# Output projection of a state-space scan: one fp32 product becomes three products of split operands, and its weights are streamed

## The chip, the cores and the metric

One core of one Trainium2 chip runs the whole kernel. The metric is the device time in microseconds (us), measured over several executions; beside it stands one execution taken by the hardware profiler. The engines are named as in the profile: PE is TensorE (matmuls; PEld is its weight load), DVE is VectorE, ACT is ScalarE, POOL is GpSimd, SP is SyncE, which here only issues transfers (DMAs).

## What is computed

A decoder layer on 2048 tokens (8 sequences of 256) with 256 channels: a Mamba-2 mixer, cross attention, and a mixture of experts. The change touches the mixer alone. Cut to what matters:

```python
proj = hidden @ W_in.T                      # z, x, B, C, dt;  inner width 4096 (64 heads of 64)
xBC  = silu(causal_conv(xBC))               # 4 taps
y    = scan(x * dt, B, C, exp(cumsum(dt*A))) + D * x
g    = y * silu(z)                          # the gated product, [tokens, 4096]
gn   = g * rsqrt(mean(g*g) + eps) * norm_w  # norm_w: 4096 values
out  = gn @ W_out.T                         # the output projection, 4096 -> 256
```

The kernel multiplies norm_w into W_out, projects g without the norm, and scales the result by the rsqrt of each token at the end of a group of tokens.

## The kernel before

`mamba_prepare` normalises the input, computes dt and its cumulative sums, splits the input weights into two float32r parts (high and low: high is the rounded value, low the rest) and stores them in HBM. Its ScalarE also multiplies norm_w into the whole output weight, 32 pieces of 128x256 (`weigh_out`, L290), which then stays in SBUF as `won`.

`mamba_scan` works through 128 steps. A step n is one tile of 128 inner channels (c = n mod 32, two heads) for one group of 512 tokens (g = n div 32). Each engine has its order written out by hand; semaphores count what is done. In its step n an engine does the following, in this order.

- PE: `transposes(n)` (L892), `x_proj(n+2)` and `z_proj(n+1)` (L873, 12 float32r products of 512 columns), `out_proj(n-1)` (L917, 4 fp32 products of 256 columns, each issued as 2 instructions), `scan(n)` (L905, into `ps_y`).
- DVE: `gate(n-1)` (L817, y from PSUM, writes `gy`), `x_times_dt(n)` (L807), `conv_x(n+1)` (L776, three instructions), `matrices(n+1)` (L786 and L789: `mat` times `cbm`, both operands and the result in SBUF), `silu_x(n+1)` (L794), `silu_z(n+1)` (L801).
- ACT: `scale_x(n+1)` (L690), `gaps(n+2)` (L702 and L704, eight instructions), `tanh_x(n+1)` (L721), `square(n-1)` (L717), `tanh_z(n+1)` (L727), `decays(n+2)` (L711).
- POOL: waits for `matrices(n+1)`, then `last_matrix(n+1)` (L663), `product(n)` (L640, g = gy times zs, writes `gT`), `add_square(n-1)` (L651, sums g*g; for the first tile of a group it is a copy, L648).
- SP: loads of the split input weights (`w_split`, 512 KB) and of the decay rows (512 KB) three steps ahead.

All of POOL's operands lie in SBUF. Of DVE's instructions in a step, L786 and L789 alone read two operands from SBUF; the others read one of theirs from PSUM. At the turn of a group DVE and POOL also compute the rsqrt and add the 512 tokens' output to `xres` (L829). At the end of the last step DVE splits the query weights for the next phase (L855).

Of the kernel before, what the change touches and what calls it, by code (L numbers as in the profile page):

```python
# [5 lines left out]
F32 = mybir.dt.float32  # L6
# [56 lines left out]
def mamba_prepare(nc, xres, ident, raw, banks, scratch, kept, first, x, w_xz, w_bc, w_dt, conv_w, conv_b, dt_bias, a_log, d_param, norm_w, w_out):  # L63

    xT_hi, xT_lo, cbm, dt, cum, cw, cb, d_ch, won, neg_half, ones, a_dram, w_dram = kept
# [23 lines left out]
    with ExitStack() as ctx:  # L89
# [16 lines left out]
        nw = sb("nw", [P, NCT])  # L106
# [17 lines left out]
        def pb(name, banks=1):  # L124
# [7 lines left out]
        wdt_loaded, wbc_loaded, small_loaded, wo_loaded = (  # L132
            sem(n) for n in ("wdt_loaded", "wbc_loaded", "small_loaded", "wo_loaded"))
# [5 lines left out]
        small_hi, small_lo, won_done = sem("small_hi"), sem("small_lo"), sem("won_done")  # L139
# [34 lines left out]
        def _(sp):  # L174
            x_t = x.rearrange("b (n p) c -> p (b n) c", p=P)
            for g in range(NG):
# [6 lines left out]
                     (nw[:], norm_w)]  # L183
# [9 lines left out]
            sp.dma_start(won[:], w_out).then_inc(wo_loaded, 16)  # L193
# [60 lines left out]
        def _(act):  # L254
# [32 lines left out]
            def weigh_out(c):  # L287
                if c == 0:
                    act.wait_ge(wo_loaded, 16)
                act.activation(won[:, c, :], won[:, c, :], ACT.Copy, scale=nw[:, c:c + 1]).then_inc(won_done, 1)  # L290

# [27 lines left out]
            for j in range(5, 9):  # L319
                for c in range((j - 5) * 8, (j - 4) * 8):  # L320
                    weigh_out(c)
                w_high(j)
            tanh(0)
            w_high(9)
            for n in range(2):
                act.wait_ge(aT_ready, n + 1)
                act.activation(aT[:, n * TG:(n + 1) * TG], ps_dt[:, n * TG:(n + 1) * TG], ACT.Copy)\
                    .then_inc(aT_done, 1)
# [217 lines left out]
def mamba_scan(nc, xres, ident, banks, scratch, kept, first, retired, next_loads, keys, split):  # L546

    xT_hi, xT_lo, cbm, dt, cum, cw, cb, d_ch, won, neg_half, ones, a_dram, w_dram = kept
# [3 lines left out]
    NCT = won.shape[1]  # L552
# [9 lines left out]
    TRI = 3 * P  # L562

    with ExitStack() as ctx:
# [7 lines left out]
        a_all = [a_first] + [sb(f"a_all{u}", [P, HPT, TG])[:] for u in range(1, 3)]  # L572
        mat = sb("mat", [P, 3, HPT, BG * TRI])
# [11 lines left out]
        def pb(name, banks=1):  # L585
# [9 lines left out]
        (x_scaled, gap_done, exp_done, x_tanh, z_tanh, g_squared) = (  # L595
            sem(n) for n in ("x_scaled", "gap_done", "exp_done", "x_tanh", "z_tanh", "g_squared"))
        mat_last = sem("mat_last")
        (conv_step, x_silu, z_silu, xdt_done, mat_done, gy_done, g_done, sum_mean, x_added) = (
            sem(n) for n in ("conv_step", "x_silu", "z_silu", "xdt_done", "mat_done", "gy_done", "g_done",
                             "sum_mean", "x_added"))  # L600
        (g_summed, r_veps, r_done) = (sem(n) for n in ("g_summed", "r_veps", "r_done"))
# [5 lines left out]

        block = ctx.enter_context(nc.Block())

        @block.sync  # L610
        def _(sp):
            sp.sem_clear(retired)
            for n in range(N):
# [6 lines left out]
                if n >= 3:  # L620
                    sp.wait_ge(gap_done, HPT * (n - 2))
                if n >= 1:
                    row = a_dram[g, c * HPT:(c + 1) * HPT, :].rearrange("h t -> (h t)")
                    sp.dma_start(a_all[u].rearrange("p h t -> p (h t)"), row.partition_broadcast(P))\
                        .then_inc(a_loaded[u], 16)
                if n == 8:
                    sp.wait_ge(w_stored[2], 16 * (NCT // 8))
                    sp.wait_ge(w_stored[3], 16 * (NCT // 8))
                    for dst, src, loaded in next_loads:
                        sp.dma_start(dst, src).then_inc(loaded, 16)  # L630

# [1911 lines left out]
```

## Time and profile before

| | before |
|---|---|
| median of 3 runs | 1694.83 us (1694.37 to 1695.42) |
| the profiled execution's own time | 1693.64 us |
| its span | 1691.9 us |
| busy share PE, DVE, ACT, POOL | 95%, 74%, 72%, 43% |

The span is what the profiler saw between the first and the last instruction, so 1.7 us of the profiled execution lie around it. The page divides the span into stages with quite different limits: about 86 us of `mamba_prepare`, 870 us of `mamba_scan`, then attention and experts. The shares above are means over all of them, so the argument has to be made inside the scan, and there inside one step.

### The profile page before, as it was taken

The page shows a single profiled execution, that of the slowest core. Times are in us where ns is not written, and L with a number is a line of the kernel's source. Part 1 is how long each engine was busy: PE and PEld are TensorE (multiplying, and loading weights), DVE is VectorE, ACT ScalarE, POOL GpSimd, SP SyncE. Part 2 cuts the span into 40 slices and gives each one's busy share as a digit, 9 for nine tenths or more (in the row PEclk, how much of TensorE's full clock was granted, in tenths as well). Part 3 has the DMA queues.
Part 4 walks back from the last instruction along what each step waited for, and adds up shares of the span by engine and source line. Part 5 has one row for each costly group of instructions (what it writes and reads, how often), then busy time and mean ns, then how long its engine had stood idle before and what let it go on. Part 6 is the DMA issues. An engine that isn't in the chain of part 4 may idle for free. (4 is left out here: it accounts for less than half of the span.)

```text
span 1691.9 us, 29098 instructions
## 1 busy us (share of the span) xinstructions
PE 1603.2 (95%) x9864; PEld 1281.0 (76%) x9864; DVE 1254.0 (74%) x2044; ACT 1217.1 (72%) x2518; POOL 731.8 (43%) x601
## 2 busy tenths in 40 slices
PE   5479999999999999999999999999969999999999
PEld 3357777777777777777777677878757889999888
DVE  7969999999999999999999865567666533333355
ACT  4679999999999999999999576566624324444331
POOL 1425555555555555555555511311113653334460
PEclk9689999999999999999999999999989999999999
DMA  8966444444444444444444100000215323222231
GB/s 324 389 231 253 164 152 172 150 158 167 151 172 152 154 171 150 173 151 153 172 150 150 55 1 13 14 14 14 72 75 190 117 96 133 90 91 95 79 99 51
DMA packets 78078, 226.62 MB, mean 134 GB/s; under 512 B 9072, under 2 KB 32880, under 8 KB 76272
## 3 DMA queue, kind: packets, MB, share of 16 engines
q1 hardware_dynamic: 72272, 198.67, 32.9%
q0 software_dynamic: 5664, 26.09, 4.4%
q8 instruction: 85, 1.39, 0.3%
q14 instruction: 57, 0.47, 0.1%
HBM read 187.77 MB, written 36.96 MB: 133 GB/s over the span
## 5 line engine op out<-in xcount | busy, mean ns | idle before, releaser
L776 DVE SCALAR_TENSOR_TENSOR m_xc<-banks,k_cw,m_xc 128x510 f32<-128x510 f32 (+2 forms) x384 | 285.4, 743 | 16.6 <-ACT m_xc L690 7.2
L917 PE MATMUL m_ps_out<-k_won,m_gT 128*128 128x256 f32 x1024 | 242.3, 379 | 3.2 <-POOL m_gT L640 2.0
L873 PE MATMUL banks<-pair_hi,m_wxz 128*128 128x512 f32 x680 | 241.7, 406 | 2.5 <-DMA m_wxz<-w_split 2.5
L640 POOL TENSOR_TENSOR m_gT<-m_gy,m_zs 128x512 f32<-128x512 f32 x128 | 166.4, 1300 | 172.3 <-DVE m_gy L817 171.4
L663 POOL TENSOR_TENSOR m_mat<-m_mat,k_cbm 128x384 f32<-128x384 f32 x128 | 129.8, 1014 | 230.6 <-DVE m_mat L789 216.8
L917 PEld LDWEIGHTS m_ps_out<-k_won,m_gT 128*128 128x128 f32 x1024 | 193.6, 190 | 36.1 <-POOL m_gT L640 3.3
L905 PE MATMUL m_ps_y<-m_mat,m_xdt 128*64 128x256 f32 (+1 forms) x2048 | 194.7, 332 | 0.0
L711 ACT ACTIVATE m_mat<-m_mat 128x1536 f32<-128x1536 f32 x128 | 188.6, 1473 | 0.0
L905 PEld LDWEIGHTS m_ps_y<-m_mat,m_xdt 128*64 128x64 f32 x2048 | 126.8, 136 | 80.0 <-issue 42.3
L702 ACT ACTIVATE m_mat<-m_a_all,k_cum 128x256 f32<-128x256 f32 x340 | 170.6, 502 | 0.0
L651 POOL TENSOR_TENSOR m_g_sum<-m_g_sum,m_g_sq 128x512 f32<-128x512 f32 x124 | 162.4, 1310 | 5.3 <-ACT m_g_sq L717 5.1
L873 PEld LDWEIGHTS banks<-pair_hi,m_wxz 128*128 128x128 f32 x680 | 127.6, 188 | 31.3 <-DMA m_wxz<-w_split 3.5
L2384 PE MATMUL f_gu<-f_room,f_gT_hi 128*128 x468 | 141.3, 363 | 2.4 <-issue 2.4
L2243 DVE TENSOR_TENSOR f_h<-f_silu,f_gu 128x256 f32<-128x256 f32 (+1 forms) x117 | 44.0, 376 | 129.7 <-PE f_ps_hT L2394 107.4
L817 DVE SCALAR_TENSOR_TENSOR m_gy<-m_xs,logits,m_ps_y 128x512 f32<-128x512 f32 x128 | 95.6, 747 | 55.1 <-PE m_ps_y L905 54.7
L873 PE MATMUL banks<-pair_lo,m_wxz 128*128 128x512 f32 x340 | 134.4, 395 | 0.0
L704 ACT ACTIVATE m_mat<-m_a_all,k_cum 128x128 f32<-128x128 f32 x340 | 134.1, 394 | 0.0
L873 PE MATMUL banks<-pair_hi,k_w_first 128*128 128x512 f32 x344 | 127.3, 411 | 3.8 <-PEq L89 2.5
L786 DVE TENSOR_TENSOR m_mat<-m_mat,k_cbm 128x768 f32<-128x768 f32 x128 | 121.4, 949 | 2.8 <-ACT m_mat L711 2.8
L1175 POOL TENSOR_TENSOR a_q_r<-a_q_ve,a_neg_half 128x32 f32<-128x32 f32 x8 | 43.4, 5426 | 168.9 <-DVE a_q_ve L1368 168.9
L2309 PE MATMUL f_gu<-pair_hi,f_room 128*128 128x512 f32 x320 | 104.7, 404 | 6.5 <-DVE f_room L2064 6.3
L690 ACT ACTIVATE m_xc<-banks,logits,k_cw 128x512 f32<-128x512 f32 x128 | 98.3, 768 | 8.9 <-PE banks L873 8.9
(325 smaller groups left out, 3774.9 us busy)
## 6 DMA issues: line engine op xcount, KB each, us to landing
m_wxz<-w_split SPq DMA_DIRECT2D x85, 512.0 KB, 3.4
m_a_all<-a_by_head SPq DMA_DIRECT2D x85, 512.0 KB, 4.4
k_w_first<-w_split SPq DMA_DIRECT2D x43, 512.0 KB, 3.3
k_a_first<-a_by_head SPq DMA_DIRECT2D x43, 512.0 KB, 4.2
w_split<-p_w_hl SPq DMA_DIRECT2D x15, 1024.0 KB, 8.6
raw<-in_w_gate_up POOLq DMA_DIRECT2D x9, 1280.0 KB, 6.5
raw<-in_w_xz SPq DMA_DIRECT2D x16, 512.0 KB, 7.1
raw<-in_w_down POOLq DMA_DIRECT2D x9, 640.0 KB, 7.9
```

Source lines behind the costliest of these rows:

```text
L640: pool.tensor_tensor(gT[:, n % 2, :], gy[:, n % 2, :], zs[:, n % 2, :], ALU.mult).then_inc(g_done, 1)
L651: pool.tensor_tensor(g_sum[:, g % 2, :], g_sum[:, g % 2, :], g_sq[:, n % 2, :], ALU.add)\
L663: pool.tensor_tensor(mat[:, n % 3, 1, TRI:2 * TRI], mat[:, n % 3, 1, TRI:2 * TRI], cbm[:, n // NCT * BG + 1, :], ALU.mult).then_inc(mat_la ...
L702: act.activation(mat[:, u, h, b * TRI:b * TRI + SEQ], a_all[u][:, h, b * SEQ:(b + 1) * SEQ], ACT.Relu, bias=cum[:, t, head:head + 1], scal ...
L704: last = act.activation(mat[:, u, h, b * TRI + SEQ:(b + 1) * TRI], a_all[u][:, h, b * SEQ + P:(b + 1) * SEQ], ACT.Relu, bias=cum[:, t + 1, ...
L711: act.activation(mat[:, n % 3], mat[:, n % 3], ACT.Exp, scale=-1.0).then_inc(exp_done, 1)
L776: dve.scalar_tensor_tensor(out=out[:, :, k:], in0=ps[:, :, 0:SEQ - k], scalar=cw[:, c, TAPS - 1 - k:TAPS - k], in1=out[:, :, k:], op0=ALU. ...
L786: dve.tensor_tensor(mat[:, u, 0, :], mat[:, u, 0, :], cbm[:, g * BG:(g + 1) * BG, :].rearrange("p b t -> p (b t)"), ALU.mult)\
L873: last = pe.matmul(ps[:, :], w, a, start=m == 0, stop=m == len(terms) - 1)
L905: last = pe.matmul(ps_y[h * HD:(h + 1) * HD, b * SEQ + at:(b + 1) * SEQ], xdt[:, 2 * b + half, h * HD:(h + 1) * HD], mat[:, u, h, b * TRI ...
L917: last = pe.matmul(ps_out[:, q * HID:(q + 1) * HID], gT[:, n % 2, q * P:(q + 1) * P], won[:, c, :], start=c == 0 and q % 2 == 0, stop=c == ...
L2384: last = pe.matmul(ps_gu[m % 4][:, 0:2 * (i1 - i0)], a, w, start=q == 0, stop=q == len(terms) - 1)
```

## The change

The output projection gets two float32r parts of each operand: g is split into `gT_hi` and `gT_lo`, and the weighted output weight into `won[..., 0]` (high) and `won[..., 1]` (low); the three products hi*hi, hi*lo and lo*hi replace the fp32 one. POOL makes both parts of g. The output weight no longer stays in SBUF: a ring of 4 tiles (`WON`) is kept. In the first group (steps 1 to 32) the raw weight tile is loaded, ACT makes the high part and DVE the low one, and SP stores both parts in HBM; in groups 1 to 3 SP streams both parts back (256 KB a step). `out_proj` moves from step n+1 to step n+2. The 32 weightings and the 4 MB load leave `mamba_prepare`. Several semaphores are merged, and a sign moves from ACT's `scale=-1.0` into the stored rows, which changes no instruction's size.

```diff
 mamba_prepare:
-            sp.dma_start(won[:], w_out).then_inc(wo_loaded, 16)
-                for c in range((j - 5) * 8, (j - 4) * 8):
-                    weigh_out(c)
 mamba_scan, sync:
+            def move_won(n):
+                kept_c, c = n - WON - 2, n - WON
+                if n > WON:
+                    sp.wait_ge(won_moved, 16 * won_moves(n - 1))
+                if 0 <= kept_c < NCT:
+                    sp.wait_ge(won_lo_done, kept_c + 1)
+                    sp.dma_start(won_dram[kept_c], won[:, kept_c % WON]...)
+                if 0 <= c < NCT:
+                    if c >= WON:
+                        sp.wait_ge(won_lo_done, c - WON + 1)
+                    sp.dma_start(won_raw[:, c % WON], w_out[:, c, :]).then_inc(won_moved, 16)
+                elif c >= NCT:
+                    sp.wait_ge(out_ready, c - WON + 1)
+                    sp.dma_start(won[:, c % WON]..., won_dram[c % NCT])
...
-                    sp.wait_ge(gap_done, HPT * (n - 2))
+                    sp.wait_ge(exp_done, n - 2)
...
+                if n >= WON:
+                    move_won(n)
 mamba_scan, gpsimd:
+            def high_part(n):
+                pool.wait_ge(g_done, n + 1)
+                if n >= 2:
+                    pool.wait_ge(out_ready, n - 1)
+                pool.tensor_copy(gT_hi[:, n % 2, :], gT[:, n % 2, :]).then_inc(gT_hi_done, 1)
+
+            def low_part(n):
+                pool.wait_ge(gT_hi_done, n + 1)
+                pool.tensor_tensor(gT_lo[:, n % 2, :], gT[:, n % 2, :], gT_hi[:, n % 2, :].bitcast(F32),
+                                   ALU.subtract).then_inc(gT_lo_done, 1)
...
                     last_matrix(n + 1)
+                if n >= 1:
+                    high_part(n - 1)
+                    low_part(n - 1)
                 if n < N - 1:
                     product(n)
...
                 if n == N - 1:
                     product(n)
+                    high_part(n)
 mamba_scan, scalar:
+            def won_high(c):
+                act.wait_ge(won_moved, 16 * won_moves(c + WON))
+                if c >= WON:
+                    act.wait_ge(out_ready, c - WON + 1)
+                act.activation(won[:, c % WON, 0], won_raw[:, c % WON], ACT.Copy, scale=nw[:, c:c + 1])\
+                    .then_inc(won_hi_done, 1)
...
-                if n == N - 1:
-                    wq_high()
-                if n >= 1:
-                    square(n - 1)
+                square(n - 1)
                 if n + 1 < N:
                     tanh_z(n + 1)
                 if n + 2 < N:
                     decays(n + 2)
+                if n <= NCT:
+                    won_high(n - 1)
+                if n == N - 1:
+                    wq_high()
 mamba_scan, vector:
+            def won_low(c):
+                dve.wait_ge(won_hi_done, c + 1)
+                dve.scalar_tensor_tensor(out=won[:, c % WON, 1], in0=won_raw[:, c % WON], scalar=nw[:, c:c + 1],
+                                         in1=won[:, c % WON, 0].bitcast(F32), op0=ALU.mult, op1=ALU.subtract)\
+                    .then_inc(won_lo_done, 1)
...
                     silu_z(n + 1)
+                if 1 <= n <= NCT:
+                    won_low(n - 1)
...
             wq_low(1, 0)
+            last_low_part()
             wq_low(1, 1)
 mamba_scan, tensor:
             def out_proj(n):
                 g, c = n // NCT, n % NCT
-                pe.wait_ge(g_done, n + 1)
+                pe.wait_ge(gT_lo_done, n + 1)
+                if g == 0:
+                    pe.wait_ge(won_lo_done, c + 1)
+                else:
+                    pe.wait_ge(won_moved, 16 * won_moves(n + WON))
...
+                terms = [(gT_hi, 0), (gT_hi, 1), (gT_lo, 0)]
                 for q in range(TPG):
-                    last = pe.matmul(ps_out[:, q * HID:(q + 1) * HID], gT[:, n % 2, q * P:(q + 1) * P],
-                                     won[:, c, :], start=c == 0 and q % 2 == 0, stop=c == NCT - 1,
-                                     skip_group_check=True)
+                    for m, (a, part) in enumerate(terms):
+                        last = pe.matmul(ps_out[:, q * HID:(q + 1) * HID], a[:, n % 2, q * P:(q + 1) * P],
+                                         won[:, n % WON, part], start=c == 0 and q % 2 == 0 and m == 0,
+                                         stop=c == NCT - 1 and m == len(terms) - 1, skip_group_check=True)
...
-                if n >= 1 and not turned:
-                    out_proj(n - 1)
+                if n >= 2 and not turned:
+                    out_proj(n - 2)
```

The order on POOL, in one step of the scan (the difference, the step before with - and the changed step with +; the waits stand in brackets):

```order
-L663 TENSOR_TENSOR m_mat<-m_mat,k_cbm 128x384 [waits m_exp_done,m_mat_done]
-L640 TENSOR_TENSOR m_gT<-m_gy,m_zs 128x512 [waits m_out_ready,m_g_squared,m_z_silu,m_gy_done]
-L651 TENSOR_TENSOR m_g_sum<-m_g_sum,m_g_sq 128x512 [waits m_g_summed,m_g_squared]
...
+L694 TENSOR_TENSOR m_mat<-m_mat,k_cbm 128x384 [waits m_exp_done,m_mat_done]
+L684 CAST k_gT_hi<-m_gT 128x512 [waits m_out_ready,m_g_done]
+L688 TENSOR_TENSOR k_gT_lo<-m_gT,k_gT_hi 128x512 [waits m_gT_hi_done]
+L660 TENSOR_TENSOR m_gT<-m_gy,m_zs 128x512 [waits m_gT_lo_done,m_g_squared,m_silu_done,m_gy_done]
+L671 TENSOR_TENSOR m_g_sum<-m_g_sum,m_g_sq 128x512 [waits m_g_summed,m_g_squared]
```

Two instructions, the cast and the subtraction, stand between `last_matrix` and `product` in every step.

The order on ACT in a step of the first group, from the last of the `gaps` on, in the changed kernel:

```order
L739 ACTIVATE m_mat<-m_a_all,k_cum 128x128
L763 ACTIVATE banks<-m_xc 128x512 [waits m_conv_step]
L759 ACTIVATE m_g_sq<-m_gT 128x512 [waits m_g_summed,m_g_done]
L769 ACTIVATE xn_ffn<-banks 128x512 [waits m_silu_done,m_z_ready]
L746 ACTIVATE m_mat<-m_mat 128x1536 [waits m_gap_done]
L752 ACTIVATE k_won<-k_won_raw,logits 128x256 [waits m_won_moved]
L725 ACTIVATE m_xc<-banks,logits,k_cw 128x512 [waits m_silu_done,m_x_ready]
```

The high part of the weight (L752) is the last thing of the step, behind `decays` (L746); before, `decays` was followed by the next step's `scale_x`.

The order on DVE at the same place, from the last instruction of the convolution to the first of the next one, in the changed kernel:

```order
L819 SCALAR_TENSOR_TENSOR m_xc<-banks,k_cw,m_xc 128x2x253 [waits m_conv_step]
L829 TENSOR_TENSOR m_mat<-m_mat,k_cbm 128x768 [waits m_exp_done]
L832 TENSOR_TENSOR m_mat<-m_mat,k_cbm 128x384
L837 SCALAR_TENSOR_TENSOR m_xs<-banks,m_xc 128x512 [waits m_tanh_done]
L844 SCALAR_TENSOR_TENSOR m_zs<-xn_ffn,banks 128x512 [waits m_g_done,m_tanh_done]
L865 SCALAR_TENSOR_TENSOR k_won<-k_won_raw,logits,k_won 128x256 [waits m_won_hi_done]
L860 SCALAR_TENSOR_TENSOR m_gy<-m_xs,logits,m_ps_y 128x512 [waits m_g_done,m_y_ready]
L850 TENSOR_TENSOR m_xdt<-banks,k_dt 128x512 [waits m_t_ready]
L819 SCALAR_TENSOR_TENSOR m_xc<-banks,k_cw,m_xc 128x2x255 [waits m_x_scaled]
```

The low part (L865) has come in between `silu_z` and `gate`, with a wait for ACT's L752; `gate`, `x_times_dt` and the next convolution are queued behind it. After step 32 the rows L752 and L865 are absent and the rest is as before.

## Rows read from the trace of the kernel before

**Rows 1.** The page's first lines: span, busy time and share of each engine.

```profile
span 1691.9 us, 29098 instructions
PE 1603.2 (95%) x9864; PEld 1281.0 (76%) x9864; DVE 1254.0 (74%) x2044; ACT 1217.1 (72%) x2518; POOL 731.8 (43%) x601
```

**Rows 2.** Busy time by stretch: prepare (two stretches), steady scan; count of instructions in brackets.

```profile
core 0: us, PE busy (x) PEld busy (x) DVE busy (x) ACT busy (x) POOL busy (x), PEclk, DMA share, GB/s
36.00:55.00 19.00, 2.06 (x9) 1.32 (x7) 18.62 (x17) 19.00 (x41) 0.00 (x0) 0.64 0.93 341
55.00:85.00 30.00, 19.67 (x62) 13.46 (x63) 26.33 (x40) 16.73 (x23) 19.88 (x9) 0.73 1.02 394
...
500.00:941.00 441.00, 439.97 (x2678) 339.08 (x2676) 404.99 (x610) 426.21 (x861) 238.03 (x204) 1.00 0.44 154
```

**Rows 3.** Timeline of PE in a steady step: start, duration, what.

```profile
603.36 1.89 PE L917 MATMUL m_ps_out<-k_won,m_gT 128*128 128x256 f32 x8
605.18 1.52 PE L905 MATMUL m_ps_y<-m_mat,m_xdt 128*64 128x256 f32 x16
```

**Rows 4.** Timeline of DVE in the same step; idle time and releaser in square brackets.

```profile
600.17 0.75 DVE L817 SCALAR_TENSOR_TENSOR m_gy<-m_xs,logits,m_ps_y 128x512 f32<-128x512 f32 x1 [0.48 <-PE m_ps_y L905]
...
601.44 2.30 DVE L776 SCALAR_TENSOR_TENSOR m_xc<-banks,k_cw,m_xc 128x510 f32<-128x510 f32 x3
603.65 0.95 DVE L786 TENSOR_TENSOR m_mat<-m_mat,k_cbm 128x768 f32<-128x768 f32 x1
604.52 0.55 DVE L789 TENSOR_TENSOR m_mat<-m_mat,k_cbm 128x384 f32<-128x384 f32 x1
...
606.75 0.75 DVE L817 SCALAR_TENSOR_TENSOR m_gy<-m_xs,logits,m_ps_y 128x512 f32<-128x512 f32 x1 [0.48 <-PE m_ps_y L905]
```

**Rows 5.** Timeline of ACT in the same step.

```profile
603.77 0.60 ACT L721 ACTIVATE banks<-m_xc 128x512 f32<-128x512 f32 x1
...
605.30 1.47 ACT L711 ACTIVATE m_mat<-m_mat 128x1536 f32<-128x1536 f32 x1
606.68 0.77 ACT L690 ACTIVATE m_xc<-banks,logits,k_cw 128x512 f32<-128x512 f32 x1
```

**Rows 6.** Timeline of ACT: `scale_x` of tiles 2, 3 and 32.

```profile
110.56 0.76 ACT L690 ACTIVATE m_xc<-banks,logits,k_cw 128x512 f32<-128x512 f32 x1
116.88 0.77 ACT L690 ACTIVATE m_xc<-banks,logits,k_cw 128x512 f32<-128x512 f32 x1
...
307.94 0.77 ACT L690 ACTIVATE m_xc<-banks,logits,k_cw 128x512 f32<-128x512 f32 x1
```

**Rows 7.** Timeline of POOL in the steady step.

```profile
601.00 1.29 POOL L640 TENSOR_TENSOR m_gT<-m_gy,m_zs 128x512 f32<-128x512 f32 x1 [1.41 <-DVE m_gy L817]
602.25 1.29 POOL L651 TENSOR_TENSOR m_g_sum<-m_g_sum,m_g_sq 128x512 f32<-128x512 f32 x1
605.15 1.01 POOL L663 TENSOR_TENSOR m_mat<-m_mat,k_cbm 128x384 f32<-128x384 f32 x1 [1.61 <-DVE m_mat L789]
```

**Rows 8.** Timeline of DVE, then POOL, at the scan's start and end.

```profile
98.20 0.96 DVE L786 TENSOR_TENSOR m_mat<-m_mat,k_cbm 128x768 f32<-128x768 f32 x1 [0.72 <-ACT m_mat L711]
99.08 1.35 DVE L789 TENSOR_TENSOR m_mat<-m_mat,k_cbm 128x384 f32<-128x384 f32 x1
...
98.32 1.70 POOL L663 TENSOR_TENSOR m_mat<-m_mat,k_cbm 128x384 f32<-128x384 f32 x1 [12.05 <-ACT m_mat L711]
...
944.95 4.46 POOL L651 TENSOR_TENSOR m_g_sum<-m_g_sum,m_g_sq 128x512 f32<-128x512 f32 x2
```

**Rows 9.** Groups of POOL by line and shape: busy us, mean ns of one, idle before.

```profile
L1894 POOL CAST f_room<-raw 128x1280 fp32r<-128x1280 f32 x8 | 10.1, 1258 | 0.0
...
L648 POOL COPY m_g_sum<-m_g_sq 128x512 f32<-128x512 f32 x4 | 2.5, 618 | 0.0
```

**Rows 10.** Groups by line (ACT in prepare, DVE at turns); last row: timeline of PE.

```profile
L290 ACT ACTIVATE k_won<-k_won,p_nw 128x256 f32<-128x256 f32 x32 | 13.2, 508 | 0.0
...
L829 DVE SCALAR_TENSOR_TENSOR xres<-m_ps_out,m_r_out,xres 128x256 f32<-128x256 f32 x12 | 4.9, 474 | 0.0
...
1397.43 1.86 PEld L2404 LDWEIGHTS f_ps_y<-f_room 128*128 128x128 f32 x15
```

More of the change, by code:

```diff
@@ L131, in mamba_prepare @@
         x_loaded = [sem(f"x_loaded{g}") for g in range(NG)]
[L132 to L133 removed]
+        wdt_loaded, wbc_loaded, small_loaded = (
+            sem(n) for n in ("wdt_loaded", "wbc_loaded", "small_loaded"))
         w_loaded = [sem(f"w_loaded{u}") for u in range(RING)]
@@ L326, in _ @@
                 act.wait_ge(aT_ready, n + 1)
-                act.activation(aT[:, n * TG:(n + 1) * TG], ps_dt[:, n * TG:(n + 1) * TG], ACT.Copy)\
+                act.activation(aT[:, n * TG:(n + 1) * TG], ps_dt[:, n * TG:(n + 1) * TG], ACT.Copy, scale=-1.0)\
                     .then_inc(aT_done, 1)
@@ L630, in _ @@
                         sp.dma_start(dst, src).then_inc(loaded, 16)
+            for n in range(N, N + WON):
+                move_won(n)
         @block.gpsimd
@@ L720, in tanh_x @@
                 act.wait_ge(conv_step, (n + 1) * CONV)
-                act.activation(ps_x[n % 2][:, :], xc[:, n % 2, :], ACT.Tanh).then_inc(x_tanh, 1)
+                act.activation(ps_x[n % 2][:, :], xc[:, n % 2, :], ACT.Tanh).then_inc(tanh_done, 1)
             def tanh_z(n):
@@ L725, in tanh_z @@
                 if n >= 1:
-                    act.wait_ge(z_silu, n)
-                act.activation(thz, ps_z[:, :], ACT.Tanh, scale=0.5).then_inc(z_tanh, 1)
+                    act.wait_ge(silu_done, 2 * n)
+                act.activation(thz, ps_z[:, :], ACT.Tanh, scale=0.5).then_inc(tanh_done, 1)
             def wq_high():
@@ L837, in _ @@
             for n in range(N):
-                turned = n % NCT == 1 and n > 1
                 if n >= 1:
                     gate(n - 1)
-                if turned:
+                if n % NCT == 1 and n > NCT:
                     mean_out(n // NCT - 1)
@@ L845, in _ @@
                     conv_x(n + 1)
-                if turned:
+                if n % NCT == 2 and n > NCT:
                     add_out(n // NCT - 1)
@@ L953, in _ @@
                     context_keys(0)
-                turned = n % NCT == 1 and n > 1 or n == N - 1
-                if n >= 1 and not turned:
-                    out_proj(n - 1)
+                turned = n % NCT == 2 and n > NCT
+                if n >= 2 and not turned:
+                    out_proj(n - 2)
                 scan(n)
                 if turned:
-                    out_proj(n - 1)
+                    out_proj(n - 2)
                 if n % NCT == 0 and n > 0:
                     sums(n // NCT - 1)
+            out_proj(N - 2)
             context_keys(1)
+            context_keys(2)
             out_proj(N - 1)
             sums(NG - 1)
-            context_keys(2)
             context_keys(3)
@@ L973, in mamba_phase @@
     NH = 2 * NCT
+    WON = 4
     with ExitStack() as ctx:
```

121 lines of the change are left out of this document (67 added, 54 removed).

## Prediction, made before the changed kernel ran

> **What bounds the kernel now.** I began with the page's first lines [rows 1]. PE is busy 95% of the span, which suggests that cheaper products help; but the mean runs over stages with different limits, so I took busy time by stretch next. In the steady scan (the last of [rows 2]) PE is busy 439.97 of 441.00 us, ACT 426.21, DVE 404.99 and POOL 238.03. PE comes first, but ACT is 3% behind, and that is the room that a faster PE has.
>
> The timeline of one step says the same in detail. From gate to gate [rows 4] a step is 606.75 - 600.17 = 6.58 us. DVE's one idle time is 0.48 us, waiting for PE's scan. ACT's own length shows where nothing holds it up: at the scan's start `scale_x` follows `scale_x` after 116.88 - 110.56 = 6.32 us [rows 6]. So PE sets 6.57, ACT would set 6.32, and DVE without its wait 6.58 - 0.48 = 6.10. POOL has three instructions in a step and waits 1.41 and 1.61 us before two of them [rows 7]; what the reader is to see there is where the idle time lies. POOL ends `add_square` at 603.54, DVE runs its two `matrices` instructions from 603.65 to 605.07 [rows 4], POOL begins `last_matrix` at 605.15. POOL rests exactly while DVE multiplies two operands out of SBUF.
>
> That matters because the two engines do not run such work side by side. In the first step they met [rows 8]: L786 ran from 98.20 to 99.16, POOL's L663 was issued at 98.32 and took 1.70 instead of 1.01, ending 0.86 after L786; then L789, issued at 99.08, took 1.35 instead of 0.55 and ended 0.41 after L663 did. At the end of the scan, beside DVE's L855 (also two SBUF operands), two `add_square` took 4.46 us instead of 2.58. The blocked one starts when the other ends, and merely 0.14 or 0.15 us of its fixed time is hidden. Instructions of DVE with one operand in PSUM do not do this: L776 lies under POOL's L640 and L651 [rows 4, 7] at its usual 2.30 for three.
>
> The Trainium skill, page "SBUF — State Buffer", section "Who interferes with whom", has this as an exclusive lock on a shared pair of ports, taken by a DVE instruction with two SBUF inputs against a GpSimd instruction that reads SBUF. By that rule the new POOL work of this change isn't free however idle POOL looks; the rows above agree.
>
> **The change part by part.**
>
> *PE.* Removed: 8 instructions from 603.36 to 605.18, 1.82 us [rows 3]. Added: 12 float32r products of 256 columns. The same form runs in the experts' stage, 15 weight loads in 1.86 us, 0.12 each [rows 10], so 12 take about 1.45. PE gains 0.37 a step, down to 6.2. Since ACT needs 6.32, no more than 0.25 of it could ever show.
>
> *POOL, groups 1 to 3.* Added in every step: the cast and the subtraction. The cast of 512 columns isn't in the trace; the nearest rows are the copy of 512 (0.618) and the cast of 1280 (1.258) [rows 9], so 0.49 (in proportion) to 0.62; I take 0.62, the row of its own width. The subtraction is a product's form, 1.29. Now POOL's chain after `matrices` is longer than DVE's way to the next `matrices`. From the end of L789: `last_matrix` begins 0.08 later [rows 7, 4] and takes 1.01; the cast 0.62; the subtraction waits for the cast, which I put at the same 0.08, and takes 1.29; `product` and `add_square` 1.29 each. Instructions that follow without a wait start 0.04 before the end of the one ahead (602.25 against 602.29 [rows 7]), three times here. Sum 0.08 + 1.01 + 0.62 + 0.08 + 3 x 1.29 - 3 x 0.04 = 5.54. DVE's way from the end of L789 to its next L786 is 6.10 less the 1.42 of the pair (603.65 to 605.07), 4.68. So L786 is issued 0.9 us before POOL is done, under `add_square`, which began at 4.29, before it, and is blocked. L786 ends 0.95 - 0.14 = 0.81 after `add_square`, L789 0.47 later (605.07 - 604.60), and `last_matrix` waits for both. That closes a loop: 5.54 + 0.81 + 0.47 = 6.82 us, longer than PE's 6.57 now. Lost: 0.25 a step in 95 steps, 24 us. Both ends: nothing blocked gives 6.32, a gain of 0.25; a cast as slow as a two-operand instruction (1.29) gives 7.49, a loss of 0.92.
>
> By the Trainium skill's rule just named (the loser blocks for the whole of the other's instruction, nothing hidden) the loop would be 6.96, and 13 us more would be lost; rows 8 show the 0.14 hidden, so I leave it out.
>
> *The first group.* Here ACT makes the high part of the weight as the last thing of a step, DVE waits for it with the low part, and `gate`, `x_times_dt` and the next convolution are queued behind that wait. That is a loop through ACT and DVE. From the convolution's end (603.74 [rows 4]) to `tanh_x` 0.03, from there to the end of `decays`' slot 606.68 - 603.77 = 2.91 [rows 5], then the high part, 0.51 (L290 is the same work [rows 10]), and 0.05 to be seen: DVE can issue the low part at 3.50. It has two SBUF operands, 256 columns; nearest row L829, 0.47 [rows 10]. POOL's subtraction lies there: L789 ends 1.33 after the convolution, and by the sum above the subtraction ends 0.08 + 1.01 + 0.62 + 0.08 + 1.29 - 0.04 = 3.04 later, at 4.37, and began at 3.08, ahead of the low part. So this ends at 4.37 + 0.47 - 0.14 = 4.70; `gate` starts 0.08 earlier, the convolution 1.27 after `gate` (601.44 - 600.17), and takes 2.30: 8.19 us a step. Before, the same steps took (307.94 - 110.56) / 30 = 6.58 [rows 6]. Lost: 1.61 in 31 steps (the first one hides it behind ACT's prologue), 50 us. Without the block the low part ends at 3.97 and a step takes 7.46, still 0.88 more: 27 us. ACT's added 0.4 alone would give 6.72.
>
> *Prepare.* ACT loses 32 instructions, 13.2 us [rows 10], and the DMAs 4.2 MB. I cost this at nothing: in 36 to 55 us, where they ran, DVE is busy 18.62 of 19 us [rows 2] with the chain that ends this stage, and they lay beside it; in 55 to 85 it is busy 26.33 of 30. The DMA share is 1.02 there, so if transfers set the end, up to 4 us (DVE's idle time) could come back.
>
> *Streaming.* 256 KB a step more beside 1 MB, at a DMA share of 0.44 [rows 2]; SP issues up to two more transfers a step. Each has two steps to land. Nothing; if it were late, PE would wait in `out_proj`, with `scan` and then DVE's `gate` behind it.
>
> *Turns and tail.* At a turn DVE adds output, as before. After the last step the cast and subtraction of tile 126, the cast of 127 and a subtraction on DVE stand on the way to the last sum: 0.62 + 1.29 + 0.62 + about 0.7 = 3 us.
>
> Sum: 24 + 50 + 3 = 77 us on the profiled execution's 1693.64, 1771. The median of the runs is 1.2 higher: 1772.
>
> **The rivals.**
>
> *The low part isn't blocked in the first group* (POOL's subtraction comes after it): 7.46 a step, 1772 - 23 = 1749. For it: 0.4 us decide the order. Against it: POOL's chain starts at the same L789 and has fixed lengths.
>
> *No block at all in the steady steps* (it was seen in the first and the last steps alone, since POOL rested in the rest): 6.32 a step from 33 on, 24 us gained, 27 lost in the first group, 3 in the tail: 1701. Against it, rows 8.
>
> *Faster.* PE's gain shows and the first group costs nothing. The mechanism would be that DVE's wait for ACT's high part is covered: the low part needs to be ready when `silu_z` ends (2.5 after the convolution) and comes at 3.50, so 1.0 us would have to go. It decides when that gap and the block both fall away: 0.25 in 126 steps, 1695 - 31 = 1664.
>
> *POOL is slower still*: a cast at two-operand price, or blocks that also catch DVE between L786 and L789. From half of that, 0.3 a step, to all of it, 0.67, in 126 steps: 1810 to 1856.
>
> **How the numbers follow.** Forecast (both loops) 0.63, its own range 1755 to 1790; first group unblocked 0.13; no block 0.09; faster 0.05; slower still 0.10. Leaving out the last three would leave 0.24 outside, so the range takes in the lower part of the slower case and all of the second: 1743 to 1800. Times within 0.2% (3.4 us) can't be told from no change here. Of the 0.09 I give 0.03 to within and 0.05 to slower, 0.01 to faster. Slower 0.91, same 0.03, faster 0.06.
>
> **What would show it.** In the changed profile L829 (was L786) should take about 1.7 to 1.8 instead of 0.95, ending some 0.81 after POOL's L671; gate to gate 6.8 in the later groups, PE and ACT both with idle time, POOL busy some 85%. In the first group gate to gate 8.2, L865 taking about 1.2 with an idle time before it that ACT's L752 ends. PE's L980 should take 1.4 to 1.5 in all. Prepare should end within 4 us of where it did. I am wrong if L829 stays at 0.95 beside a busy POOL, if L865 is issued before POOL's L688, or if PE waits in `out_proj` for a transfer.

## The result, and the profile after

| | before | after |
|---|---|---|
| median (4 runs each) | 1694.6 us (1693.2 to 1695.4) | 1768.8 us (1768.1 to 1771.3) |
| profiled execution, its span | 1693.64, 1691.9 | 1771.26, 1769.5 |

The changed kernel is slower: ratio 1.0445, 95% interval 1.0432 to 1.0458. The page's first lines, to be held against [rows 1]:

```profile
span 1769.5 us, 30975 instructions
PE 1580.4 (89%) x10376; PEld 1293.7 (73%) x10376; DVE 1352.4 (76%) x2077; ACT 1219.8 (69%) x2518; POOL 964.8 (55%) x856
```

PE lost 23 us of busy time and POOL gained 233. DVE gained 98 us with only 33 more instructions. Of these, the 32 low parts of the weight are busy 36.3 us in all, about 1.15 us each. The largest share lies in an old instruction that takes longer: L829 is busy 191.8 us where L786, the same work, was busy 121.4. Busy time by stretch, as in [rows 2]:

```profile
core 0: us, PE busy (x) PEld busy (x) DVE busy (x) ACT busy (x) POOL busy (x), PEclk, DMA share, GB/s
36.00:55.00 19.00, 2.83 (x13) 1.94 (x11) 18.62 (x17) 7.86 (x9) 0.00 (x0) 0.71 0.88 315
...
500.00:941.00 441.00, 410.55 (x2855) 331.35 (x2852) 436.46 (x592) 415.38 (x838) 347.09 (x327) 1.00 0.56 194
```

In the steady scan DVE alone is busy nearly all the time (436.46 of 441 us, 99%). Its timeline shows why (compare [rows 4]):

```profile
680.02 0.73 DVE L860 SCALAR_TENSOR_TENSOR m_gy<-m_xs,logits,m_ps_y 128x512 f32<-128x512 f32 x1
...
683.48 1.75 DVE L829 TENSOR_TENSOR m_mat<-m_mat,k_cbm 128x768 f32<-128x768 f32 x1
685.16 0.54 DVE L832 TENSOR_TENSOR m_mat<-m_mat,k_cbm 128x384 f32<-128x384 f32 x1
...
686.82 0.73 DVE L860 SCALAR_TENSOR_TENSOR m_gy<-m_xs,logits,m_ps_y 128x512 f32<-128x512 f32 x1
```

POOL's timeline in the same step (compare [rows 7]):

```profile
679.92 0.62 POOL L684 CAST k_gT_hi<-m_gT 128x512 fp32r<-128x512 f32 x1
680.62 1.29 POOL L688 TENSOR_TENSOR k_gT_lo<-m_gT,k_gT_hi 128x512 fp32r<-128x512 f32 x1
681.87 1.30 POOL L660 TENSOR_TENSOR m_gT<-m_gy,m_zs 128x512 f32<-128x512 f32 x1
683.12 1.30 POOL L671 TENSOR_TENSOR m_g_sum<-m_g_sum,m_g_sq 128x512 f32<-128x512 f32 x1
685.78 1.00 POOL L694 TENSOR_TENSOR m_mat<-m_mat,k_cbm 128x384 f32<-128x384 f32 x1 [1.36 <-DVE m_mat L832]
```

L829 is issued at 683.48, while POOL's L671 runs until 684.42. It shows 1.75 us where the same instruction took 0.95 before, and ends at 685.23, 0.81 after L671. Gate to gate is 6.80 us. PE now waits 0.47 us for the transposes' operand, and its output projection runs from 682.86 to 684.37, where `scan` begins, 1.51 us:

```profile
679.55 0.66 PE L949 MATMUL banks<-ident,m_xs 128*128 128x128 f32 x4 [0.47 <-DVE m_xs L837]
...
682.86 0.39 PE L980 MATMUL m_ps_out<-k_won,k_gT_hi 128*128 128x256 f32 x2
...
684.37 1.52 PE L962 MATMUL m_ps_y<-m_mat,m_xdt 128*64 128x256 f32 x16
```

The first group is another loop. DVE's timeline there, from the last of a convolution to the next L829:

```profile
202.84 0.74 DVE L819 SCALAR_TENSOR_TENSOR m_xc<-banks,k_cw,m_xc 128x506 f32<-128x506 f32 x1
203.50 0.95 DVE L829 TENSOR_TENSOR m_mat<-m_mat,k_cbm 128x768 f32<-128x768 f32 x1
...
207.06 1.15 DVE L865 SCALAR_TENSOR_TENSOR k_won<-k_won_raw,logits,k_won 128x256 fp32r<-128x256 f32 x1 [0.95 <-ACT k_won L752]
208.13 0.74 DVE L860 SCALAR_TENSOR_TENSOR m_gy<-m_xs,logits,m_ps_y 128x512 f32<-128x512 f32 x1
208.78 0.68 DVE L850 TENSOR_TENSOR m_xdt<-banks,k_dt 128x512 f32<-128x512 f32 x1
209.38 2.30 DVE L819 SCALAR_TENSOR_TENSOR m_xc<-banks,k_cw,m_xc 128x510 f32<-128x510 f32 x3
211.60 0.95 DVE L829 TENSOR_TENSOR m_mat<-m_mat,k_cbm 128x768 f32<-128x768 f32 x1
```

POOL there:

```profile
206.63 1.29 POOL L688 TENSOR_TENSOR k_gT_lo<-m_gT,k_gT_hi 128x512 fp32r<-128x512 f32 x1
208.94 1.30 POOL L660 TENSOR_TENSOR m_gT<-m_gy,m_zs 128x512 f32<-128x512 f32 x1 [1.02 <-DVE m_gy L860]
```

DVE waits 0.95 us for ACT's high part, then the low part (L865) is issued 0.86 us before POOL's subtraction ends (207.92), takes 1.15 us and ends 0.29 after it. L829 is unblocked here, 0.95, since the delayed DVE gives POOL time to finish. A step is 8.10 us.

ACT's timeline, `scale_x` of tiles 2 and 32, says how much each part of the scan lost (compare [rows 6]):

```profile
111.34 0.76 ACT L725 ACTIVATE m_xc<-banks,logits,k_cw 128x512 f32<-128x512 f32 x1
...
352.76 0.77 ACT L725 ACTIVATE m_xc<-banks,logits,k_cw 128x512 f32<-128x512 f32 x1
```

Tile 2 comes 0.8 us later than before; from tile 2 to tile 32 it is 241.4 instead of 197.4 us, 44.0 more; from tile 32 to tile 127 654.8 instead of 628.9, 26.0 more (worked out from the starts of that instruction for the two tiles in each trace); and from there to the first instruction of the next phase on DVE 5.3 more. Together 76 of the 77.6 us by which the profiled executions differ; that of the changed kernel was the slowest of its four, and the medians differ by 74.2 us.

### The profile page after: what moved, and what is told of

Its sections match the earlier page's. It is cut to its first block and busy times, and to the rows that moved or that the text cites. A ratio compares the mean times of both kernels' runs of the same rounds, so it can differ in the third digit from the quotient of the medians.

```text
span 1769.5 us, 30975 instructions
## 1 busy us (share of the span) xinstructions
PE 1580.4 (89%) x10376; PEld 1293.7 (73%) x10376; DVE 1352.4 (76%) x2077; ACT 1219.8 (69%) x2518; POOL 964.8 (55%) x856
## 5 line engine op out<-in xcount | busy, mean ns | idle before, releaser
L980 PE MATMUL m_ps_out<-k_won,k_gT_hi 128*128 128x256 f32 x1024 | 188.8, 282 | 5.8 <-DVE k_gT_lo L872 2.6
L829 DVE TENSOR_TENSOR m_mat<-m_mat,k_cbm 128x768 f32<-128x768 f32 x128 | 191.8, 1498 | 2.8 <-ACT m_mat L746 2.8
L746 ACT ACTIVATE m_mat<-m_mat 128x1536 f32<-128x1536 f32 x128 | 188.6, 1474 | 0.0
L980 PEld LDWEIGHTS m_ps_out<-k_won,k_gT_hi 128*128 128x128 f32 x1024 | 166.4, 190 | 20.0 <-DVE k_gT_lo L872 3.5
L949 PE MATMUL banks<-ident,m_xs 128*128 128x128 f32 x512 | 85.2, 290 | 98.4 <-DVE m_xs L837 98.4
L688 POOL TENSOR_TENSOR k_gT_lo<-m_gT,k_gT_hi 128x512 fp32r<-128x512 f32 x127 | 164.6, 1296 | 10.2
L671 POOL TENSOR_TENSOR m_g_sum<-m_g_sum,m_g_sq 128x512 f32<-128x512 f32 x124 | 161.8, 1305 | 2.3 <-ACT m_g_sq L759 2.3
L949 PEld LDWEIGHTS banks<-ident,m_xs 128*128 128x128 f32 x512 | 54.8, 142 | 128.3 <-DVE m_xs L837 127.4
L980 PE MATMUL m_ps_out<-k_won,k_gT_lo 128*128 128x256 f32 x512 | 144.2, 282 | 0.0
```

What stands on the lines that cost most here:

```text
L671: pool.tensor_tensor(g_sum[:, g % 2, :], g_sum[:, g % 2, :], g_sq[:, n % 2, :], ALU.add)\
L688: pool.tensor_tensor(gT_lo[:, n % 2, :], gT[:, n % 2, :], gT_hi[:, n % 2, :].bitcast(F32), ALU.subtract).then_inc(gT_lo_done, 1)
L746: act.activation(mat[:, n % 3], mat[:, n % 3], ACT.Exp, scale=-1.0).then_inc(exp_done, 1)
L829: dve.tensor_tensor(mat[:, u, 0, :], mat[:, u, 0, :], cbm[:, g * BG:(g + 1) * BG, :].rearrange("p b t -> p (b t)"), ALU.mult)\
L949: last = pe.transpose(ps_t[:, q * P:(q + 1) * P], xs[:, n % 2, q * P:(q + 1) * P], ident)
L980: last = pe.matmul(ps_out[:, q * HID:(q + 1) * HID], a[:, n % 2, q * P:(q + 1) * P], won[:, n % WON, part], start=c == 0 and q % 2 == 0 an ...
```

## Experiments

All kernels start from the changed one unless the text says otherwise. The medians beside them are of 4 to 11 runs, against the kernel before on the same chip (1692.8 to 1694.9). Not all experiments ran on one chip, so a difference between two of them is good to about 1 us; the ratios leave the chip out.

**1. An operand from PSUM.** The kernel leaves out the multiplication by `cbm` from tile 34 on: DVE multiplies `mat` by what lies in a PSUM bank instead. Only the place of one operand is meant to change.

```diff
+                if n > NCT + 1:
+                    t_part = ps_t[:, 0:TRI]
+                    dve.tensor_tensor(batches(mat[:, u, 0, :]), batches(mat[:, u, 0, :]),
+                                      t_part.unsqueeze(1).broadcast_to([P, BG, TRI]), ALU.mult).then_inc(mat_done, 1)
+                    dve.tensor_tensor(mat[:, u, 1, 0:TRI], mat[:, u, 1, 0:TRI], t_part, ALU.mult)...
```

> From tile 34 on DVE's two matrices instructions read a PSUM bank in place of cbm (the result is wrong from there on), so they have one operand in SBUF; everything else, POOL's new work included, is as in the changed kernel. Theory (DVE's instruction with two SBUF operands and POOL's instructions exclude each other): the first of them takes 0.95 to 1.0 us again instead of 1.75 beside a POOL that is as busy as before, gate to gate falls from 6.81 to the lengths of PE and ACT, 6.32 to 6.40, in 94 steps: 1768.8 - 42 = 1727 (1722 to 1732). Rival (POOL's load slows DVE whatever its operands, or POOL's own chain of 5.5 us with its waits sets the step): the instruction stays at 1.7 or the step stays at 6.8, 1765 to 1770.

Measured 1729.6 us, ratio 1.0199 (1.0182 to 1.0216). DVE, then POOL, in its steady step:

```profile
682.67 0.94 DVE L831 TENSOR_TENSOR m_mat<-m_mat,banks 128x768 f32<-128x768 f32 x1
...
689.00 0.95 DVE L831 TENSOR_TENSOR m_mat<-m_mat,banks 128x768 f32<-128x768 f32 x1
```

```profile
681.98 1.30 POOL L671 TENSOR_TENSOR m_g_sum<-m_g_sum,m_g_sq 128x512 f32<-128x512 f32 x1
...
688.31 1.30 POOL L671 TENSOR_TENSOR m_g_sum<-m_g_sum,m_g_sq 128x512 f32<-128x512 f32 x1
```

The multiplication is again issued under POOL's L671 (682.67, while that runs until 683.28) and takes 0.94. The step is 6.33. POOL does the same work as in the changed kernel, 5.3 us a step in both. So it is not POOL's load as such nor the length of its chain that costs 0.47 us a step, but that DVE's instruction takes both operands from SBUF beside it.

**2. PE's part undone.** In groups 1 to 3 one fp32 product of the two high parts takes the place of the three; the products with the low parts are left out.

```diff
+                if g > 0:
+                    for q in range(TPG):
+                        last = pe.matmul(ps_out[:, q * HID:(q + 1) * HID], gT_hi[...].bitcast(F32),
+                                         won[:, n % WON, 0].bitcast(F32), ...)
```

> In groups 1 to 3 PE makes one fp32 product of the two high parts again instead of three (the low parts are still made, streamed and waited for, but not used, so precision is lost). That undoes PE's share of the change alone. Theory (POOL and DVE set 6.81): PE goes back to 6.57 of its own, its wait for the transposes' operand shrinks from 0.47 to 0.23, the step stays at 6.81 and the time at 1769 (1766 to 1772). Rival (PE's gain of 0.24 shows in the step and the new loop costs more than I think): 95 x 0.24 = 23 us slower, 1792.

Measured 1772.1 us (1767.7 to 1773.0), ratio 1.0446 (1.0429 to 1.0464), that of the changed kernel and at the upper end of the expected range. PE's output projection takes 1.82 us again and the step stays, at 6.79:

```profile
681.72 1.89 PE L980 MATMUL m_ps_out<-k_won,k_gT_hi 128*128 128x256 f32 x8
683.54 1.52 PE L962 MATMUL m_ps_y<-m_mat,m_xdt 128*64 128x256 f32 x16
```

The cheaper products were worth nothing in the kernel as changed.

**3. The whole of `mat` on DVE.** One instruction of 1536 columns replaces DVE's two and POOL's `last_matrix`. POOL begins its cast when it is over.

```diff
-                dve.tensor_tensor(mat[:, u, 0, :], ...)
-                dve.tensor_tensor(mat[:, u, 1, 0:TRI], ...)
+                cb_all = cbm[:, g * BG:(g + 1) * BG, :].rearrange("p b t -> p (b t)")
+                dve.tensor_tensor(mat[:, u], mat[:, u],
+                                  cb_all.unsqueeze(1).broadcast_to([P, HPT, BG * TRI]), ALU.mult)...
-                    pool.wait_ge(mat_done, HPT * (n + 2))
-                    last_matrix(n + 1)
+                        pool.wait_ge(mat_done, n + 2)
```

> DVE multiplies the whole of mat (128x1536) in one instruction and POOL's last_matrix is gone; POOL begins the cast when DVE's instruction is over. Theory (the sum of the work that excludes each other sets the step): POOL's chain falls from 5.54 to 4.53, the multiplication is issued 4.7 after the last one ended, so nothing blocks; it takes about 1.75, DVE alone is 6.10 + 0.33 = 6.43, and this is the step in groups 1 to 3, 6.4 to 6.5: 33 to 39 us back; in the first group 7.6 to 7.8 instead of 8.1, 10 to 15 us back. 1768.8 - 47 = 1722 (1714 to 1732). Rival (DVE has no idle time in the changed steady step, so DVE is the bound and takes on more work): 6.81 + 0.33 = 7.14, 1769 + 31 = 1800.

Measured 1713.1 us, ratio 1.0108 (1.0091 to 1.0125): DVE took on more work, and the kernel became 56 us faster. DVE and POOL in the steady step:

```profile
683.13 1.75 DVE L822 TENSOR_TENSOR m_mat<-m_mat,k_cbm 128x1536 f32<-128x1536 f32 x1
...
689.47 1.75 DVE L822 TENSOR_TENSOR m_mat<-m_mat,k_cbm 128x1536 f32<-128x1536 f32 x1
```

```profile
681.79 1.31 POOL L670 TENSOR_TENSOR m_g_sum<-m_g_sum,m_g_sq 128x512 f32<-128x512 f32 x1
684.94 0.61 POOL L683 CAST k_gT_hi<-m_gT 128x512 fp32r<-128x512 f32 x1 [1.84 <-DVE m_mat L822]
```

POOL has ended at 683.10, 0.03 before DVE begins: nothing blocks. The step is 6.34, below my 6.43; the DVE work of a step without any wait is a little shorter than the 6.10 that I had taken (without a wait an instruction's row begins 0.08 before the end of the one ahead). The time is 9 us better than expected and just below the range of 1714 to 1732: in the traces 41.7 us came back in groups 1 to 3 (33 to 39 expected) and 16.6 in the first group (10 to 15 expected). The rival, by which a DVE without idle time can't take on work, is out. A blocked instruction counts as busy: 0.8 us of DVE's busy time in each steady step of the changed kernel was waiting.

In the first group the step is 7.47. DVE, then POOL:

```profile
208.67 0.52 DVE L856 SCALAR_TENSOR_TENSOR k_won<-k_won_raw,logits,k_won 128x256 fp32r<-128x256 f32 x1 [0.61 <-ACT k_won L744]
```

```profile
207.62 1.29 POOL L687 TENSOR_TENSOR k_gT_lo<-m_gT,k_gT_hi 128x512 fp32r<-128x512 f32 x1
```

The low part is issued late in the subtraction, 0.24 before it ends, and takes 0.52 us, where it takes 0.48 by itself (experiment 8). So the block costs it 0.04 us at most, and the loop through ACT sets this step.

**4. The high part early.** ACT makes it right after `scale_x`.

```diff
                     scale_x(n + 1)
+                if n <= NCT:
+                    won_high(n - 1)
...
-                if n <= NCT:
-                    won_high(n - 1)
```

> ACT makes the high part of the weight right after scale_x instead of at the end of its step; all else as in the changed kernel. Theory (DVE's wait for ACT's last instruction closes the loop of the first group): the wait before L865 is gone, only its own 0.3 to 0.5 us stays in the loop of POOL and DVE, 6.81 + 0.35 = 7.15 (7.0 to 7.3) instead of 8.10 in some 29 steps: 28 us back, 1741 (1736 to 1746). Rival (the exclusion with POOL's subtraction costs the first group most of its time, wherever the high part is made): at best 0.3 of the 1.5 us comes back, 7.8, 1760. Groups 1 to 3 stay at 6.81 by both.

Measured 1759.1 us, ratio 1.0372 (1.0355 to 1.039): 10 us instead of 28. ACT's timeline shows a new wait:

```profile
208.34 0.51 ACT L752 ACTIVATE k_won<-k_won_raw,logits 128x256 fp32r<-128x256 f32 x1 [0.66 <-DMA k_won_raw<-in_w_out]
```

The load of a raw tile is the last that SP issues in a step, and at the start of ACT's next one it hasn't landed. The steps vary between 6.7 and 9.7 us, and one takes 13.7. The exchange of one wait for another decides nothing; hence the next experiment.

**5. The high part in the middle** of ACT's step, between `gaps` and `tanh_x`.

```diff
                     gaps(n + 2, 1)
+                if n <= NCT:
+                    won_high(n - 1)
                 if n + 1 < N:
                     tanh_x(n + 1)
```

> As the run with the early high part, but ACT makes it between the gaps and tanh_x, 3 us later in its step, where the raw weight tile has landed. Theory (the first group's loop was DVE's wait for ACT's last instruction; what the early high part lost again was its own wait for the DMA): no ACT wait for a DMA in the first group, DVE's L865 without a wait ahead of it, 7.1 to 7.25 us a step instead of 8.10, so 29 x 0.92 = 27 us back, 1742 (1737 to 1747). Rival (the low part on DVE and its meeting with POOL's subtraction is what costs): no better than the early one, 1757 to 1762.

Measured 1734.9 us, ratio 1.0244 (1.0228 to 1.026): 34 us below the changed kernel, more than the 27 expected and below the range of 1737 to 1747. DVE, then POOL, in a step of the first group:

```profile
246.03 0.80 DVE L865 SCALAR_TENSOR_TENSOR k_won<-k_won_raw,logits,k_won 128x256 fp32r<-128x256 f32 x1
```

```profile
245.93 0.62 POOL L684 CAST k_gT_hi<-m_gT 128x512 fp32r<-128x512 f32 x1
246.63 1.35 POOL L688 TENSOR_TENSOR k_gT_lo<-m_gT,k_gT_hi 128x512 fp32r<-128x512 f32 x1
```

Without the wait for ACT the low part is issued before the subtraction. It waits for the cast (ends 0.28 after it), and the subtraction then loses only 0.06. Step 6.86. So the place of one ACT instruction of 0.5 us had cost the first group 1.24 us a step, together with the blocking that it led to. One step takes 12.97 us here (experiment 8 is about it).

**6. Both edits, 3 and 5.** (The two diffs above, nothing else.)

> Both: the whole of mat multiplied by DVE in one instruction, and the high part of the weight in the middle of ACT's step. Theory: groups 1 to 3 stay at 6.34; in the first group nothing is exclusive at the same time, so DVE's own 6.34 + 0.45 = 6.79 or ACT's 6.72 sets the step instead of 7.47: 29 x 0.68 = 20 us below 1713, 1693 (1689 to 1698), about the kernel before. Rival (the loop through ACT closes at another place): first group at 7.2 or above, 1705 to 1713.

Measured 1711.3 us, ratio 1.0105 (1.009 to 1.0121). This was a miss: 2 us below experiment 3 instead of 20, and only 0.5 by the ratios. The first group stays at 7.47. DVE, then POOL:

```profile
202.62 1.23 DVE L856 SCALAR_TENSOR_TENSOR k_won<-k_won_raw,logits,k_won 128x256 fp32r<-128x256 f32 x1
```

```profile
202.26 1.30 POOL L687 TENSOR_TENSOR k_gT_lo<-m_gT,k_gT_hi 128x512 fp32r<-128x512 f32 x1
```

The wait for ACT is gone, but with `last_matrix` off POOL its subtraction starts 1 us earlier, now 0.36 before the low part is issued. The low part ends 0.29 after the subtraction whether it was issued early or late. In experiment 3 the loop through ACT had given 7.47 us; with that loop gone the block gives 7.47 too. That the two are equally long is chance, and it hid the gain of the edit. I had counted lengths and left out who comes first.

**7. The control: the kernel before with edit 3.**

> The kernel before, with the whole of mat multiplied by DVE and without POOL's last_matrix. Theory (the kernel before is bound by PE's 6.57; what the move gave the changed kernel was room on the shared resource): DVE goes from 6.10 to 6.34 of its own, PE's 6.57 stays, 1695 (1692 to 1697). Rival (the move is a gain by itself, whatever the output projection): 95 x 0.24 = 23 us or more faster, 1672.

Measured 1694.2 us, ratio 1.0005 (0.9996 to 1.0014). DVE's 1536 columns take 1.75 there too, PE's output projection 1.82, the step is 6.58. The move is no gain by itself.

**8. The turn, the low part's place, and the other loads**, three kernels, each with the edits of the one before it. First PE's sums after the next transposes and DVE's mean after `x_times_dt`:

> As the run with both edits; at a turn of a group PE makes the sums after the next transposes and DVE takes their mean after x_times_dt. Theory: PE's wait of 0.5 for POOL's last sum and DVE's waits of 0.4 and 0.3 at each of three turns go, 2 to 3 us less than the run with both edits, 1690 (1686 to 1695). Rival (what is left at a turn is DVE's own 1.65 and 0.16 us of adding): no difference.

Measured 1708.4 us, ratio 1.0092 (1.0077 to 1.0107): 2.9 us less. The runs of the two kernels almost touch (lowest 1710.4, highest 1710.3), but the traces place the gain: from tile 32 to tile 127 it is 611.1 instead of 613.6 us, in the steps at the turns, as the theory says. The level is off because experiment 6 was. Then the low part in front of the multiplication of `mat`:

```diff
+                if 1 <= n <= NCT:
+                    won_low(n - 1)
                 if n + 1 < N:
                     matrices(n + 1)
                     silu_x(n + 1)
                     silu_z(n + 1)
-                if 1 <= n <= NCT:
-                    won_low(n - 1)
```

> As the run with both edits and the turn; DVE makes the low part of the weight between the convolution and the multiplication of mat instead of after silu_z. There POOL has finished add_square and waits for DVE. Theory (what kept the first group at 7.47 with the high part already there was the low part's wait for POOL's subtraction, which had begun 0.36 us ahead of it): L856's place gives about 0.48 us instead of 1.22, step 6.34 + 0.4 = 6.75 to 6.8 in the first group, 27 x 0.7 = 19 us less, 1708.4 - 19 = 1689 (1686 to 1694). Rival (the loop through ACT or PE now closes the first group): 7.2 or more, above 1700.

Measured 1699.4 us, ratio 1.0036 (1.0024 to 1.0048). The low part isn't blocked any more:

```profile
207.29 0.48 DVE L856 SCALAR_TENSOR_TENSOR k_won<-k_won_raw,logits,k_won 128x256 fp32r<-128x256 f32 x1
207.69 1.75 DVE L822 TENSOR_TENSOR m_mat<-m_mat,k_cbm 128x1536 f32<-128x1536 f32 x1
```

Steps are 6.74 and 7.00 in turn (in the second kind DVE waits 0.17 for ACT's high part), where 6.75 to 6.8 was expected. Yet only 9 of the 19 us came, and a few steps take far longer, one of them 13.13. Such a step stood in the kernel of the turn too (12.18), but there the two after it took 6.73 and 6.98 instead of 7.47; here they take 8.18 and 7.55. In the kernel of the turn the list of waits between 120 and 160 us had named the cause:

```profile
ACT k_won L744 <- DMA k_won_raw<-in_w_out: 5.3, 1, 5.3
```

SP issues five loads for the next phase, 3.8 MB, together at its step 8, and the next raw tile lies behind them: it lands 12.1 us after its issue, where 5.0 is usual. Last edit, these loads one by one from step 40 on:

```diff
-                    for dst, src, loaded in next_loads:
-                        sp.dma_start(dst, src).then_inc(loaded, 16)
+                if n >= 40 and n % 4 == 0 and n // 4 - 10 < len(next_loads):
+                    dst, src, loaded = next_loads[n // 4 - 10]
+                    sp.dma_start(dst, src).then_inc(loaded, 16)
```

> As the run before it; the five loads for the next phase (about 4 MB) are issued one by one from step 40 on instead of all together at step 8, where ACT waited 5.35 us for a raw weight tile. Theory: that one wait goes and nothing else comes, 4 to 6 us less, 1684 (1680 to 1688), below the kernel before (ratio 0.992 to 0.997). Rival (the wait only uncovers slack that the next steps use up, or the loads collide with the streaming in group 1): no difference.

Measured 1690.9 us (11 runs), ratio 0.9987 (0.9977 to 0.9996). That is 8.5 us below the one before, more than the 4 to 6 expected: tiles 2 to 32 take 207.9 instead of 217.0 us, so the steps after the long one recovered as well. The level of 1684 (1680 to 1688) was missed, since it had been worked out from the 1689 expected of the kernel before it. And the kernel before with the same spreading:

> The kernel before with the same spreading of the five loads, as a control: its own step of 8.91 at tile 9 shows a wait of 2.5 us. Theory: that is all the gain there is, 2 to 3 us, 1691 (1689 to 1693). Rival: as much as in the changed kernel, 5 us.

Measured 1691.8 us (11 runs), ratio 0.9992 (0.9983 to 1.0001): 1 us instead of 2 to 3, and the interval takes in no change. In the trace the step of 8.91 is gone, but tiles 2 to 32 take only 1.2 us less (196.2 instead of 197.4), since some steps around it had taken 6.32 and now take 6.57.

So the medians of the best arrangement of the change found here and of the same repair of the old kernel are less than 1 us apart. In the traces, groups 1 to 3 of that arrangement gain 18.5 us over the kernel before (a step is 6.34 instead of 6.57), the first group loses 10.5, and the end of the scan 3.5. These add up to a gain of 4.5 us, more than the 1.9 us between the medians: the profiled execution was the fastest of its 11 (1688.33).

## Why the prediction was right, point by point

*The time.* 1772 was forecast and 1768.8 measured. For the profiled execution it was 1771, and it took 1771.26. The parts were 24, 50 and 3 us and came out as 26.0, 44.0 and 5.3, with 0.8 at the start and 1.5 outside these stretches. That the sum fits so closely is luck in part, since errors of up to 6 us cancel. The range had a slip: its upper end, 1800, was said to take in the lower part of the slower case, which begins at 1810.

*Groups 1 to 3: right.* The loop of POOL's chain, the rest of L829 and L832 was put at 5.54 + 0.81 + 0.47 = 6.82; it is 6.80. L829 ends 0.81 after L671 as forecast, and is issued 0.94 before POOL is done (forecast 0.9). The cast takes 0.62, the row of its own width being the right one. By the full blocking of the Trainium skill (page "SBUF — State Buffer", sections "Who interferes with whom" and "Summary: rules for kernel authors") the step would be 6.96. The measured 6.80 decides: the rule gives who is blocked and by what, and experiment 1 bears it out that one operand in PSUM is enough to escape; some 0.14 us of the blocked instruction's own time is hidden, as in the meetings shown above. Of the 26.0 us, 22 are the steady steps (0.23 x 95); the first turn adds 4.4, since steps of the first group's kind reach into it, and the other two give 0.3 back each. Two of these steps, past tile 32, are still 8.10 long (3.1 us over the old ones); counted by their kind, the first group lost 47 us and groups 1 to 3 lost 23.

*First group: right in mechanism, 6 us too dear up to tile 32, 3 with the two steps behind it.* All the marks came: the low part issued 3.48 after the convolution (3.50), the subtraction begun at 3.05 (3.08) and ended at 4.34 (4.37), the low part ended at 4.63 (4.70), the step 8.10 (8.19). That is 0.09 in each of 28 steps, 2.5 us; the first two steps took 6.72 and 7.83, as the loop had to close first, 1.8 us; and the forecast's 31 steps reach past tile 32, with 30 between tiles 2 and 32.

*What makes the first group slow* was named as two things, the wait for ACT's high part and the block, and both are shown. Each by itself gives a step of 7.47: the wait for ACT in experiment 3, where the block costs 0.04, and the block in experiment 6, where the wait is gone. The forecast had the first of these as a rival, with the low part issued 3.50 after the convolution, ended at 3.97 and a step of 7.46; experiment 3 has 3.48, 4.00 and 7.47. Together they give 8.10, because the wait makes the low part late and the subtraction then holds it longer. They don't add up as separate shares: moving the high part took away both in experiment 5 (6.86), where the low part came ahead of the subtraction and waited for the cast alone, and almost nothing in experiment 6, where the subtraction came first.

*PE: the size was off.* 1.51 us instead of 1.45, the gain is 0.31 a step instead of 0.37. It made no difference (experiment 2), and where everything else was out of the way (experiments 1 and 3) the step fell to 6.33 and 6.34, as ACT's 6.32 allowed.

*Prepare and streaming: right.* Prepare costs and gains nothing: `scale_x` of tile 2 is 0.8 us later, and the first `scale_x` scatters between 90.7 and 94.0 us over the kernels above, whose prepare is the same. The 13.2 us of ACT's work and the 4.2 MB that left it were covered; DVE is as busy as before in that stretch, 18.62 of 19 us. PE never waited for a streamed weight in the steady steps. What was overlooked is that the raw tiles share the queue with the loads at step 8. In the changed kernel ACT never waits for a raw tile there, since the steps are long and ACT takes the tile last in its step. The wait was 1.3 us in experiment 3, with shorter steps, and 5.2 to 6.3 us in the kernels that take the tile earlier in ACT's step (experiments 5, 6 and the first two of 8).

*The end: 2 us too cheap.* The forecast added up the new instructions, 3 us. What it left out is that they meet instructions of the other engine with SBUF operands there. The cast of tile 127 runs beside DVE's splitting of the query weights and takes 1.49 instead of 0.61 us; the last subtraction, on DVE, is issued 0.07 after a POOL `add_square` and takes 1.73 instead of the 0.7 put down for it. That is 1.9 us. The last product is blocked as well, 2.25 us, but it was before the change too, 2.24.

*POOL's share* was put at 85%; it is 79% (347.09 of 441). That was a slip: 5.54 of 6.82 is 81%, and 0.16 of the 5.54 are waits.

## What to carry to other kernels

POOL's idle time isn't free where DVE works on two SBUF operands: add up POOL's instructions and those of DVE that take both operands from SBUF as if they were one engine's, and compare that sum with the step, as a first check. A blocked instruction looks busy and merely long, so compare its mean duration with that of the same shape elsewhere in the trace before calling the engine the bound; moving work onto the "busy" engine can be the repair. And when an instruction is moved, ask which instruction of the other engine it will now find running: issued 0.36 us behind the subtraction, the low part took 1.23 us here, and 0.48 where nothing held it.

## What the hardware showed that I had not expected

A DVE multiplication of 128x1536 in one instruction takes 1.75 us, where 768, 384 and (on POOL) 384 columns took 0.95, 0.55 and 1.01. That one cast of 0.6 us on POOL can hold up a 256-column DVE instruction (0.80 instead of 0.48) shows that POOL work with one operand blocks as well. And ACT waited 5.3 us for one small transfer, 128 KB, which landed 12.1 us after its issue instead of the usual 5.0, behind 3.8 MB of loads that nobody needed for another 800 us.
